# Leaf numbers of three routing trees: scattered to DRAM and spread by a DMA, in place of transposes on TensorE

## Chip, cores and metric

The kernel runs on one core of one Trainium2 chip. The metric is the device time of the core in microseconds; lower is better.

## What is computed

The input x is 4 x 512 tokens of width 128. The result is x + attention(xn) + ffn(xn) with xn = layernorm(x). The attention has 16 heads of width 8 and a bias by relative position. The other branch is a "fast feedforward" with four trees, q, k, v and f:

```python
def _fff(x, nw, nb, w1, b1, w2, b2, act):
    node = jnp.zeros(x.shape[:2], dtype=jnp.int32)
    for _ in range(DEPTH):                                  # 8 levels, 256 leaves
        logit = jnp.einsum('bsd,bsd->bs', x, nw[node]) + nb[node]
        node = 2 * node + 1 + (logit > 0).astype(jnp.int32)
    leaf = node - NN
    h = act(jnp.einsum('bsd,bsdl->bsl', x, w1[leaf]) + b1[leaf])   # 16 wide
    return jnp.einsum('bsl,bsld->bsd', h, w2[leaf]) + b2[leaf]

q, k, v = (_fff(xn2, ..., relu) for each of three trees)
y = xn2 + softmax(q k^T / sqrt(128)) v
ffn = y + _fff(y, f_..., gelu)
```

Each token takes a path through a tree to one of 256 leaves and is multiplied by the small matrices of that leaf.

## The kernel before, in words

**Leaves in blocks.** Eight leaves of 16 columns make a block of 128 columns, so a tree has 32 blocks. The tokens of a tree are sorted by block into at most 48 tiles of 128 rows (2048 tokens fill 16, and each block may leave one partly filled), and four tiles make a group: 12 groups a tree, 36 for the trees q, k and v (n = 0 to 35), 12 more for f. Within a tile every row is multiplied by its block's whole matrix, and the 16 columns of its own leaf are kept by a mask: the kernel needs for each row the leaf's number within the block (0 to 7, `part_of`), spread over all 128 partitions, since the hidden values lie there with columns on partitions and tokens along the free axis.

**Sorting.** GpSimd's `scatter(t)` (line 420) writes a tree's tokens to their slots in DRAM (`xs`) with 16 indirect DMAs of 128 rows each, a row being 128 values and, as the 129th, the leaf's number within the block (line 424 puts it into `xr[:, :, P]`). `xs` has two buffers, so tree 2 uses that of tree 0 and its scatter waits until the masks of tree 0 have been taken (line 423). GpSimd then goes on, in this order: scatter of trees 0 and 1, 32 indirect DMAs that fetch output biases (`gather_b2`), scatter of tree 2, 16 more of `gather_b2`, and then `gather(t)`, which adds each tree's results by indirect DMA (line 444) once its last store has landed.

**A group's stages** (`STAGE_AT`, line 73), each in a slot of its own:

- x: TensorE transposes the four tiles of rows (line 1185); ScalarE copies them out (line 885).
- h: TensorE multiplies them by the first matrices (line 1191); ScalarE adds the bias and applies the activation, to `hr` (line 890).
- m: TensorE transposes four tiles of the broadcast 129th column into PSUM bank 7 (lines 1193 to 1197, semaphore `mk`); VectorE compares it with `C_LEAF` and multiplies it by `hr`, to `hm` (line 739).
- y: TensorE multiplies `hm` by the second matrices into the same bank 7 (line 1201, `yy`); VectorE copies it out, to `yl` (line 744).

**The order of the work** is written out by hand as slots. An attention step (of 16, each four heads of one batch) has 20 slots; the stages of group n stand at the slots

```python
STAGE_AT = {"x": 0, "h": 2, "m": 3, "y": 5}
EVERY = 4
TREES_FROM, QK_FROM, ATT_FROM, ROUTE_FROM, F_FROM = -16, 131, 139, 174, 226
```

that is at 4n - 16 plus the stage's number, for the trees q, k and v. Slots -20 to -1 are a first step that holds only the row maxima of attention step 0. In a slot TensorE runs attention's scores (lines 1114, 1125 and 1127), at some slots the weighing of values (line 1137), and then the stage of a group that stands there; VectorE, ScalarE and TensorE all follow the same order, each its own instructions. Between two steps stands a seam: VectorE finishes the row maxima (line 707), TensorE transposes them (line 1152), VectorE subtracts them (line 713). The 16 maxima of a step run on VectorE, and TensorE may be two scores ahead.

**SP's queue** loads and stores for the groups, in `turn(n)` (line 279): rows of n+2 (line 268, waits for the mask of n), then four value loads that read the block numbers (line 273), then the weights of n+2 (four DMAs, line 277, wait for y of n), then the store of n (line 293, waits for `yl`). The rows go to `xl`, with two buffers. At a tree's first group it also waits for that tree's scatter.

Of the kernel before, what the change touches and what calls it, by code (L numbers as in the profile page):

```python
# [28 lines left out]
P = 128  # L29
# [87 lines left out]
def build(nc, x, wq, wk, wv, wp, bp, table, onehot, cf, cb, nw, nb, wl, b2, out):  # L117
# [3 lines left out]
    xs = [nc.dram_tensor(f"xs{t}", [TILES * P, ROW], F32).ap() for t in range(2)]  # L121
    ys = [nc.dram_tensor(f"ys{t}", [TILES * P, P], F32).ap() for t in range(NTREE)]

    ctx = ExitStack()
    with ctx:
        def sb(name, shape, dt=F32):
# [52 lines left out]
        part_of = sb("part_of", [P, NTREE + 1, NT], I32)  # L179
        ewc = sb("ewc", [P, NTREE + 1], I32)  # L180
# [9 lines left out]
        blks = path_bf[:, 2 * LEAVES:2 * LEAVES + 2 * (BLK + 2)].rearrange("p (h l) -> p h l", h=2)  # L190
        bitsT = flat(yt[:, 2]).bitcast(BF16).rearrange("p (h t) -> p h t", h=2)
# [26 lines left out]
            "d_ew0 d_ew1 d_ew2 d_ew3 d_x d_c d_w d_u d_b d_f d_z d_n d_sc tc pa oh hb pop nbt d_nb z_mx pl tab_in d_far aug lkc mxc "  # L218
# [8 lines left out]
        def _(sp):  # L227
# [21 lines left out]
            for t in range(2):  # L249
                sp.dma_start(xs[t].rearrange("(p a r) c -> p a (r c)", p=P, r=n),  # L250
                             zeros).then_inc(S["d_z"], 16)

# [25 lines left out]

            def turn(n, last):

                if n + 2 < last:
                    t = (n + 2) // GROUPS
                    if (n + 2) % GROUPS == 0:
                        sp.wait_ge(S[f"d_ew{t}"], 16)
                        sp.wait_ge(S["d_sc"], 16 * NT * (t + 1))
                    sp.wait_ge(S["mk"], n + 1 + CREDIT["mk"])
                    rows(n + 2)
                    block_of = blocks(n + 2)
                    sp.wait_ge(S["yy"], n + 1 + CREDIT["yy"])
                    weights(block_of, n % 2)  # L290
                t, m = divmod(n, GROUPS)
                sp.wait_ge(S["yl"], n + 1 + CREDIT["yl"])
                sp.dma_start(ys[t % NTREE][m * GT * P:(m + 1) * GT * P, :].rearrange("(t p) c -> p t c", p=P), yl[:]
                             ).then_inc(S["st"], 16)
# [3 lines left out]
            for n in range(2):  # L298
                rows(n)
                weights(blocks(n), n)  # L300
            for n in range(NTREE * GROUPS):
                turn(n, NTREE * GROUPS)
# [24 lines left out]
        def _(pool):  # L327
# [82 lines left out]
            def left_rows():  # L410

                settle(G.memset(left[:].rearrange("p a b -> p (a b)"), -1.0))
                settle(G.affine_select(left[:], left[:], [[-P, KT], [P, KT - 1]], ALU.is_ge, 0.0,
                                       base=P - SAT - 1, channel_multiplier=-1))
                pool.wait_ge(S["d_z"], 32)
                for k in range(2 * HG):
                    c = HR * (k // 2) + 25 + 3 * (k % 2)
                    G.tensor_copy(mx[:, :, c:c + 3], left[:]).then_inc(S["mxc"], 1)

            def scatter(t):  # L420
                pool.wait_ge(S["sl"], t + 1)
                if t >= 2:
                    pool.wait_ge(S["mk"], GROUPS * (t - 1) + CREDIT["mk"])
# [4 lines left out]
                pool.wait_ge(S["d_sc"], 16 * NT * (t + 1))  # L428

# [54 lines left out]
        def _(dve):  # L484
# [249 lines left out]
            def stage(k, n):  # L734
                if k == "m":
                    dve.wait_ge(S["mk"], n + 1 + CREDIT["mk"])
                    dve.wait_ge(S["hr"], n + 1 + CREDIT["hr"])
                    dve.wait_ge(S["yy"], n + CREDIT["yy"])
                    V.scalar_tensor_tensor(flat(hm[:]), bank(BB[k]), col(C_LEAF), flat(hr[:]), ALU.is_equal, ALU.mult  # L739
# [62 lines left out]
            dve.wait_ge(S["d_z"], 32)  # L802
# [170 lines left out]
        def _(pe):  # L973
# [204 lines left out]
            def stage(k, n, par):  # L1178
# [8 lines left out]
                elif k == "h":  # L1187
# [4 lines left out]
                    last.then_inc(S["hh"], 1)  # L1192
                elif k == "m":
# [4 lines left out]
                else:  # L1198
                    pe.wait_ge(S["hm"], n + 1 + CREDIT["hm"])
                    for i in range(GT):  # L1200
# [195 lines left out]
```

## Time and profile before

| | us |
|---|---|
| median of 3 runs (661.14 to 661.71) | 661.16 |
| the profiled execution, its own time | 663.95 |
| its span, first to last instruction | 662.2 |
| TensorE busy | 581.9 |
| VectorE busy | 413.3 |
| ScalarE busy | 349.2 |
| GpSimd busy | 273.0 |

All durations in the prediction are from this one profiled execution, whose own time is 2.8 us above the median. The tree stage runs from the first transposes of group 0 at 86.9 us to about 335 us; before it lie the layer norm, the routing of three trees and the first scatter. In the views, PE is TensorE's matmuls, PEld its weight loads, DVE VectorE, ACT ScalarE, POOL GpSimd and SP SyncE, whose DMA issues are marked SPq. L707 is line 707 of the kernel before. A timeline row gives start and duration in us, the engine, the line, the operation with the tiles written and read, the shape, how many instructions were merged, and in brackets the idle time ahead with what ended it.

### The profile page before, as it was taken

How to read it: one execution, taken by the hardware profiler on the slowest of the kernel's cores; microseconds unless marked ns; L12 is line 12 of the kernel's file. 1: busy time of each engine (PE TensorE's matmuls, PEld its weight loads, DVE VectorE, ACT ScalarE, POOL GpSimd, SP SyncE). 2: the span in 40 equal slices, each digit the busy share in tenths (PEclk: the TensorE clock that was granted, in tenths of full speed). 3: DMA queues.
4: the chain of work that ended last, by engine and by line, in shares of the span. 5: the costliest groups of instructions: out<-in, count | busy, mean ns of one | idle time of the engine just before them, and what ended most of it. 6: DMA issues, size and time to landing. Idle time of an engine off the chain costs nothing.

```text
span 662.2 us, 11736 instructions
## 1 busy us (share of the span) xinstructions
PE 581.9 (88%) x3641; PEld 409.5 (62%) x3641; DVE 413.3 (62%) x970; ACT 349.2 (53%) x738; POOL 273.0 (41%) x288
## 2 busy tenths in 40 slices
PE   2499878999999999999999999988598989987986
PEld 0344466768687868777766656665264767665653
DVE  3866667566676665666666665766867556746730
ACT  4533323656564646465565645423154968786633
POOL 7853576760657852840058100000077800000880
PEclk9899979999999999999999999988799999989988
DMA  7979968885768884885422100000043655632231
GB/s 213 261 174 196 301 160 214 215 225 140 209 190 216 174 207 130 187 189 156 129 36 36 26 1 0 1 1 1 1 116 69 116 132 132 173 104 58 33 65 31
DMA packets 108701, 83.05 MB, mean 125 GB/s; under 512 B 8680, under 2 KB 105840, under 8 KB 108640
## 3 DMA queue, kind: packets, MB, share of 16 engines
q1 hardware_dynamic: 93344, 69.68, 40.1%
q0 software_dynamic: 15104, 12.63, 10.4%
q8 instruction: 29, 0.48, 0.3%
q14 instruction: 32, 0.26, 0.1%
q10 hardware_dynamic: 192, 0.00, 0.0%
HBM read 57.91 MB, written 24.36 MB: 124 GB/s over the span
## 4 chain that ended last, share of the span: by engine, by line
PE 66%; DVE 11%; ACT 10%; issue 6%; DMA 3%; POOL 2%; SPq 2%; DVEq 0%; ACTq 0%
PE ps L1125 8%; PE ps L1137 8%; PE ps L1127 8%; PE ps L1114 7%; PE ps L1201 6%; PE ps L1191 6%; PE ps L1062 3%; DVE ps L707 3%; POOL xs L426 2%; PE ps L1244 2%; PE ps L1258 2%; ACT L879 2%; PE ps L1196 2%; ACT hr L890 2%; PE ps L1011 2%
## 5 line engine op out<-in xcount | busy, mean ns | idle before, releaser
L707 DVE CUSTOM_DVE_ANT_0 ps<-ps,strip 128x512 f32<-128x512 f32 x256 | 177.4, 699 | 111.3 <-PE ps L1114 106.1
L879 ACT ACTIVATE pt<-ps 128x512 f32<-128x512 f32 x256 | 150.5, 600 | 100.8 <-PE ps L1127 98.5
L1125 PE MATMUL ps<-qs,km 128*128 128x512 f32 x256 | 128.8, 503 | 8.6 <-ACT pt L879 7.5
L1114 PE MATMUL ps<-km,qs 128*128 128x512 f32 x256 | 111.7, 439 | 9.3 <-DVE mx L707 7.6
L431 POOL DMA_INDIRECT yt<-ys,slot x48 | 74.4, 1551 | 80.5 <-DMA ys<-yl 66.5
L890 ACT ACTIVATE hr<-ps,wt 128x128 f32<-128x128 f32 x192 | 54.8, 368 | 69.9 <-PE ps L1191 69.8
L1127 PE MATMUL ps<-u_lo,rev_r 128*128 128x220 f32 (+1 forms) x256 | 75.2, 294 | 0.0
L1127 PE MATMUL ps<-u_hi,rev_r 128*128 128x220 f32 (+1 forms) x256 | 73.8, 288 | 0.0
L1125 PEld LDWEIGHTS ps<-qs,km 128*128 128x128 f32 x256 | 49.9, 195 | 34.7 <-ACT pt L879 21.4
L1137 PE MATMUL ps<-pt,v_aug 128*32 128x512 f32 x512 | 69.9, 619 | 0.7 <-ACT pt L879 0.7
L426 POOL DMA_INDIRECT xs<-xr,slot x64 | 62.4, 975 | 19.7 <-issue 18.3
L1191 PEld LDWEIGHTS ps<-xTs,wt 128*128 128x128 f32 x384 | 48.3, 194 | 27.5 <-issue 20.6
L424 POOL CAST xr<-part_of 128x16 f32<-128x16 int32 x4 | 0.8, 212 | 151.4 <-DVE slot L643 126.6
L1114 PEld LDWEIGHTS ps<-km,qs 128*128 128x128 f32 x256 | 49.1, 193 | 19.5 <-DVE mx L707 13.5
L431 POOL DMA_INDIRECT xr<-ys,slot x16 | 24.8, 1553 | 86.0 <-DMA ys<-yl 81.4
L1191 PE MATMUL ps<-xTs,wt 128*128 128x128 f32 x384 | 54.6, 286 | 4.6 <-DMA wt<-in_wl 4.6
L1127 PEld LDWEIGHTS ps<-u_lo,rev_r 128*128 128x128 f32 x256 | 49.0, 192 | 11.4
L431 POOL DMA_INDIRECT yt<-in_b,leaf x48 | 45.6, 950 | 21.5 <-issue 14.0
L1127 PEld LDWEIGHTS ps<-u_hi,rev_r 128*128 128x128 f32 x256 | 50.1, 196 | 5.2 <-issue 4.1
L1201 PE MATMUL ps<-wt,hm 128*128 128x128 f32 x384 | 52.5, 281 | 0.6
L1201 PEld LDWEIGHTS ps<-wt,hm 128*128 128x128 f32 x384 | 50.2, 195 | 4.4 <-DVE hm L739 2.9
L739 DVE SCALAR_TENSOR_TENSOR hm<-ps,cst,hr 128x512 f32<-128x512 f32 x48 | 35.9, 749 | 17.1 <-ACT hr L890 11.2
(232 smaller groups left out, 891.5 us busy)
## 6 DMA issues: line engine op xcount, KB each, us to landing
wt<-in_wl SPq DMA_DIRECT2D x192, 128.5 KB
xl<-xs SPq DMA_DIRECT2D x48, 258.0 KB, 3.8
ys<-yl SPq DMA_DIRECT2D x48, 256.0 KB
xs<-mx SPq DMA_DIRECT2D x2, 3096.0 KB, 22.5
strip<-bias_bf SPq DMA_DIRECT2D x1, 3584.0 KB, 39.7
u_hi<-bias_hi SPq DMA_DIRECT2D x1, 2496.0 KB, 15.9
u_lo<-bias_lo SPq DMA_DIRECT2D x1, 2496.0 KB, 31.2
xs<-xr,slot POOLq DMA_INDIRECT x64
```

The lines of the kernel that those rows point to most:

```text
L426: pool.indirect_dma_start(out=xs[t % 2][:, :], out_offset=bass.IndirectOffsetOnAxis(ap=slot[:, t, k:k + 1], axis=0), in_=xr[:, k, :], in_o ...
L431: pool.indirect_dma_start(out=dst, out_offset=None, in_=src[:, :], in_offset=bass.IndirectOffsetOnAxis(ap=idx, axis=0), compute_op=op).the ...
L707: V.tensor_tensor_reduce(out=bank(u % 2), in0=bank(u % 2), in1=strip[:, HG * g + j, b0:b0 + NS], scale=1.0, scalar=LOWEST, op0=ALU.add, op ...
L739: V.scalar_tensor_tensor(flat(hm[:]), bank(BB[k]), col(C_LEAF), flat(hr[:]), ALU.is_equal, ALU.mult).then_inc(S["hm"], 1)
L879: A.activation(pt[:, kt % 2, j, :], bank(2 + u % 2), ACT.Exp).then_inc(S["ex"], 1)
L890: last = A.activation(hr[:, i, :], ps[:, BB[k], i * P:(i + 1) * P], ACT.Relu if n < NTREE * GROUPS else ACT.Gelu, bias=wt[:, par, i, 2 * P ...
L1114: T.matmul(bank(u % 2), qs[:, par, qt * P:(qt + 1) * P], backward(km[:, par, j, :]), start=True, stop=True).then_inc(S["p1"], 1)
L1125: T.matmul(bank(2 + u % 2), km[:, par, j, kt * P:(kt + 1) * P], qs[:, par, :], start=True, stop=False)
L1127: last = T.matmul(ps[:, 2 + u % 2, lo:hi], rev_r[:], half[:, HG * g + j, u0:u0 + hi - lo], start=False, stop=stop)
L1137: last = T.matmul(ps[HR * j:HR * j + HR, OB, :], v_aug[:, par, kt, j, :], pt[:, kt % 2, j, :], start=kt == 0, stop=kt == KT - 1)
L1191: last = T.matmul(quarter(BB[k], i), wt[:, par, i, 0:P], xTs[:, i, :], start=True, stop=True)
L1201: last = T.matmul(quarter(BB[k], i), hm[:, i, :], wt[:, par, i, P:2 * P], start=True, stop=True)
```

## The change

For the trees q, k and v the leaf's number no longer takes the way over TensorE. GpSimd writes the numbers, as bf16, with 16 more indirect DMAs a tree (2 bytes for each token) to a row in DRAM, `leaf_row[t]`, which SP has zeroed before. For each group SP loads 512 numbers of this row into all 128 partitions at once (`leaf_at`, one buffer, on the bytes of `b_pT`), and VectorE's instruction for `hm` reads them there. The stage m on TensorE is empty for these groups. Tree f keeps the transposes. Waits on `mk` become waits on `xT` (the row transposes are done) where only the read of the rows mattered; y takes over the wait for `yl`.

```diff
+    leaf_row = [nc.dram_tensor(f"leaf_row{t}", [TILES * P, 1], BF16).ap() for t in range(NTREE)]
...
+        part_bf = sb("part_bf", [P, NT], BF16)
...
+        leaf_at = path_bf[:, 0:GT * P]
...
+            for t in range(NTREE):
+                sp.dma_start(leaf_row[t].rearrange("(p a) one -> p (a one)", p=P), flat(mx[:]).bitcast(BF16)[:, 0:TILES]
+                             ).then_inc(S["d_z"], 16)
...
+            def leaves(n):
+
+                t, m = divmod(n, GROUPS)
+                sp.wait_ge(S["d_sl"], 16 * NT * (t + 1))
+                sp.dma_start(leaf_at, bass.AP(tensor=leaf_row[t].tensor, offset=m * GT * P, ap=[[0, P], [1, GT * P]])
+                             ).then_inc(S["d_at"], 16)
+
             def turn(n, last):
 
                 if n + 2 < last:
...
-                    sp.wait_ge(S["mk"], n + 1 + CREDIT["mk"])
+                    sp.wait_ge(S["xT"], n + 1)
+                    if n >= NTREE * GROUPS:
+                        sp.wait_ge(S["mk"], n - NTREE * GROUPS + 1 + CREDIT["mk"])
                     rows(n + 2)
                     block_of = blocks(n + 2)
+                if n + 1 < NTREE * GROUPS:
+                    sp.wait_ge(S["hm"], n + 1 + CREDIT["hm"])
+                    leaves(n + 1)
+                if n + 2 < last:
                     sp.wait_ge(S["yy"], n + 1 + CREDIT["yy"])
                     weights(block_of, n % 2)
...
             for n in range(2):
                 rows(n)
                 weights(blocks(n), n)
+            sp.wait_ge(S["hb"], NTREE)
+            leaves(0)
             for n in range(NTREE * GROUPS):
                 turn(n, NTREE * GROUPS)
...
-                pool.wait_ge(S["d_z"], 32)
+                pool.wait_ge(S["d_z"], 16 * (2 + NTREE))
...
             def scatter(t):
                 pool.wait_ge(S["sl"], t + 1)
                 if t >= 2:
-                    pool.wait_ge(S["mk"], GROUPS * (t - 1) + CREDIT["mk"])
+                    pool.wait_ge(S["xT"], GROUPS * (t - 1))
                 settle(G.tensor_copy(xr[:, :, P], part_of[:, t, :]))
                 for k in range(NT):
                     pool.indirect_dma_start(out=xs[t % 2][:, :], out_offset=bass.IndirectOffsetOnAxis(ap=slot[:, t, k:k + 1], axis=0),
                                             in_=xr[:, k, :], in_offset=None).then_inc(S["d_sc"], 16)
                 pool.wait_ge(S["d_sc"], 16 * NT * (t + 1))
+                if t < NTREE:
+                    settle(G.tensor_copy(part_bf[:], part_of[:, t, :]))
+                    for k in range(NT):
+                        pool.indirect_dma_start(out=leaf_row[t][:, :], out_offset=bass.IndirectOffsetOnAxis(ap=slot[:, t, k:k + 1], axis=0),
+                                                in_=part_bf[:, k:k + 1], in_offset=None).then_inc(S["d_sl"], 16)
+                    pool.wait_ge(S["d_sl"], 16 * NT * (t + 1))
...
             def stage(k, n):
                 if k == "m":
-                    dve.wait_ge(S["mk"], n + 1 + CREDIT["mk"])
+                    if n < NTREE * GROUPS:
+                        dve.wait_ge(S["d_at"], 16 * (n + 1))
+                    else:
+                        dve.wait_ge(S["mk"], n - NTREE * GROUPS + 1 + CREDIT["mk"])
                     dve.wait_ge(S["hr"], n + 1 + CREDIT["hr"])
                     dve.wait_ge(S["yy"], n + CREDIT["yy"])
-                    V.scalar_tensor_tensor(flat(hm[:]), bank(BB[k]), col(C_LEAF), flat(hr[:]), ALU.is_equal, ALU.mult
+                    V.scalar_tensor_tensor(flat(hm[:]), leaf_at if n < NTREE * GROUPS else bank(BB[k]), col(C_LEAF), flat(hr[:]), ALU.is_equal, ALU.mult
                                            ).then_inc(S["hm"], 1)
...
-            dve.wait_ge(S["d_z"], 32)
+            dve.wait_ge(S["d_z"], 16 * (2 + NTREE))
...
+                elif k == "m" and n < NTREE * GROUPS:
+                    pass
                 elif k == "m":
                     pe.wait_ge(S["yl"], n + CREDIT["yl"])
...
                 else:
                     pe.wait_ge(S["hm"], n + 1 + CREDIT["hm"])
+                    pe.wait_ge(S["yl"], n + CREDIT["yl"])
```

## Rows read from the trace of the kernel before

**Rows 1.** The page: busy time of each engine, and the granted clock in 40 slices

```profile
PE 581.9 (88%) x3641; PEld 409.5 (62%) x3641; DVE 413.3 (62%) x970; ACT 349.2 (53%) x738; POOL 273.0 (41%) x288
...
PEclk9899979999999999999999999988799999989988
```

**Rows 2.** Busy time of each engine in one stretch of the tree stage

```profile
core 0: us, PE busy (x) PEld busy (x) DVE busy (x) ACT busy (x) POOL busy (x), PEclk, DMA share, GB/s
130.00:200.00 70.00, 68.66 (x479) 52.23 (x479) 45.29 (x105) 38.95 (x94) 34.29 (x38) 1.00 0.71 190
```

**Rows 3.** Timeline of 138 to 146 us, TensorE and VectorE, groups 7 and 8

```profile
139.75 0.70 DVE L707 CUSTOM_DVE_ANT_0 ps<-ps,strip 128x512 f32<-128x512 f32 x1 [2.02 <-PE ps L1114]
...
140.37 0.75 DVE L739 SCALAR_TENSOR_TENSOR hm<-ps,cst,hr 128x512 f32<-128x512 f32 x1
...
141.17 1.16 PE L1201 MATMUL ps<-wt,hm 128*128 128x128 f32 x8
...
144.72 0.60 PE L1196 MATMUL ps<-cst,xl 128*128 128x128 f32 x4
...
145.89 0.66 PE L1152 MATMUL ps<-cst,mx 128*128 128x128 f32 x4 [0.57 <-DVE mx L707]
145.92 0.75 DVE L739 SCALAR_TENSOR_TENSOR hm<-ps,cst,hr 128x512 f32<-128x512 f32 x1
```

**Rows 4.** Timeline of TensorE alone, inside a step

```profile
125.94 0.60 PE L1196 MATMUL ps<-cst,xl 128*128 128x128 f32 x4
126.30 0.48 PE L1125 MATMUL ps<-qs,km 128*128 128x512 f32 x1
```

**Rows 5.** Groups by line, VectorE: two elementwise instructions over 512 columns

```profile
L713 DVE TENSOR_TENSOR qs<-qs,ps 128x512 fp32r<-128x512 f32 x16 | 10.9, 682 | 3.8 <-PE ps L1152 3.7
...
L641 DVE TENSOR_TENSOR pt<-pt 128x512 f32<-128x512 f32 x3 | 2.1, 692 | 0.1
```

**Rows 6.** Timeline of GpSimd: the second scatter of rows

```profile
82.61 0.21 POOL L424 CAST xr<-part_of 128x16 f32<-128x16 int32 x1 [3.99 <-DMA xs<-xr,slot]
83.10 0.98 POOL L426 DMA_INDIRECT xs<-xr,slot  x1 [0.28 <-POOL xr L424]
...
102.17 0.96 POOL L426 DMA_INDIRECT xs<-xr,slot  x1 [0.30 <-issue]
106.57 1.00 POOL L431 DMA_INDIRECT yt<-in_b,leaf  x1 [3.43 <-DMA xs<-xr,slot]
```

**Rows 7.** DMA issues of the whole run, then those of 86 to 112 us: last column us to landing

```profile
xTs<-in_nw SPq DMA_DIRECT2D x1, 128.0 KB, 2.3
xTs<-in_nb SPq DMA_DIRECT2D x1, 128.0 KB, 3.2
...
xl<-xs SPq DMA_DIRECT2D x4, 258.0 KB, 4.6
```

**Rows 8.** Timeline of VectorE: hm of groups 0 and 2

```profile
95.69 0.75 DVE L739 SCALAR_TENSOR_TENSOR hm<-ps,cst,hr 128x512 f32<-128x512 f32 x1
...
106.34 0.75 DVE L739 SCALAR_TENSOR_TENSOR hm<-ps,cst,hr 128x512 f32<-128x512 f32 x1
```

**Rows 9.** List of waits, 112 to 340 us: engine waited for, us in total, times, longest

```profile
POOL yt L431 <- DMA ys<-yl: 66.5, 2, 47.4
...
POOL xr L424 <- PE ps L1196: 20.8, 1, 20.8
```

**Rows 10.** Timeline of SP's DMA issues: first step, then around group 7

```profile
100.99 0.56 SPq L268 DMA_DIRECT2D xl<-xs  x1
104.64 1.93 SPq L277 DMA_DIRECT2D wt<-in_wl  x4
...
138.51 0.43 SPq L293 DMA_DIRECT2D ys<-yl  x1
140.03 0.38 SPq L268 DMA_DIRECT2D xl<-xs  x1
142.80 1.93 SPq L277 DMA_DIRECT2D wt<-in_wl  x4
```

More of the change, by code:

```diff
@@ L217, in build @@
         S = {n: ctx.enter_context(nc.semaphore(n)) for n in (
-            "d_ew0 d_ew1 d_ew2 d_ew3 d_x d_c d_w d_u d_b d_f d_z d_n d_sc tc pa oh hb pop nbt d_nb z_mx pl tab_in d_far aug lkc mxc "
+            "d_ew0 d_ew1 d_ew2 d_ew3 d_x d_c d_w d_u d_b d_f d_z d_n d_sc tc pa oh hb pop nbt d_nb d_sl d_at z_mx pl tab_in d_far aug lkc mxc "
             "sl tick rt_in rt_out ones ln_m ln_r ln_sub ln_sq ln_out xT_ps xT_sb xnT_sb tab_ps tab_sb v_ps v_sb lg bit oh5 rk rt id wsc "
```

## The prediction

> **What bounds the kernel now.** I read the page first: TensorE is busy 581.9 us of 662.2 [rows 1]. That is an average, so I then read the busy time of a stretch of the tree stage, where the change acts: from 130 to 200 us TensorE is busy 68.66 of 70 us, at a granted clock of 1.00 (its 2.4 GHz level), while VectorE has 45.29 and ScalarE 38.95 [rows 2]. There TensorE is the bound, and an instruction taken from it can shorten the run. The timeline around the seam between two attention steps shows the exception: TensorE idles 0.57 us before the transposes of the row maxima (line 1152), because VectorE's last maximum isn't ready [rows 3]. The same happens at each seam of the tree stage.
>
> Durations below are of the profiled execution (663.95 us, span 662.2, so 1.75 lie outside the span). The median of the runs is 661.16, 2.8 lower; I put the sum on the median.
>
> **What is removed.** Each of the 36 groups of trees 0 to 2 loses four transposes on TensorE. The four start at 125.94 and the next matmul at 126.30: 0.355 us a group [rows 4]. All 36 would be 12.8 us, but not all count. The mask stage of group n stands at slot 4n - 13 and a step has 20 slots, so the groups fall into kinds. In groups 8, 13, 18, 23, 28 and 33 the mask transposes stand last in a step: in group 8 they start at 144.72, and behind them line 1152 waits for the maximum until 145.89 [rows 3]. Without them it waits the longer, so the gain is 0. In groups 7, 12, 17, 22, 27 and 32 VectorE computes hm at 140.37, straight behind the maximum that began at 139.75, and TensorE's second matmul (line 1201) starts at 141.17, once hm is done [rows 3]. What holds hm there is VectorE's own order, not the transposes: gain 0. Groups 0 to 3 lie in the first attention step, where VectorE and the weight loads set the pace: gain 0. The other 20 give 20 x 0.355 = **-7.1 us**. The bounds are -12.8 (all 36 count) and -5 (some third of the 20 goes back into waits for VectorE and ScalarE).
>
> The instruction for hm now reads bf16 from SBUF in place of f32 from PSUM. An elementwise instruction over 512 columns takes 692 ns with both tensors in SBUF and 682 with one in PSUM [rows 5], so this is priced at 0. The Trainium skill (VectorE: DVE Perf Modes, section "The TRN2 errata") gives 58 + FD cycles from SBUF and 120 + FD from PSUM. By that each hm would be 65 ns shorter, an estimate, and the sum some 0.8 us lower over the twelve groups where hm is on the path. The rows show nothing of it.
>
> **What is added on GpSimd.** Behind each scatter of rows now stand a cast, 16 more indirect DMAs and a wait for their landing. The second row scatter is the model: cast at 82.61, DMAs from 83.10 to 102.17 (1.27 us apart), and the instruction after the wait at 106.57, in all 24.0 us [rows 6]. In the changed kernel this block for tree 0 stands exactly where the second scatter stood, so its leaf numbers are in DRAM at 106.6, and SP can't load them before. The load that spreads them (128 partitions x 1 KB) lands 2.3 us after its issue (as a plain 128 KB load did), 3.2 (as a row broadcast to all partitions) or 4.6 (as the loads of xl at this time) [rows 7]. I take 3.5, near the broadcast, since the second row scatter then runs beside it. hm of group 0 started at 95.69 [rows 8]. Now it starts at 110.1: **+14.4 us** (13.2 to 15.5). Queued behind this wait on VectorE are the row maxima of the first step, and TensorE, at most two scores ahead of them, stands still too. The slots are one order on every engine, so nothing later fills the hole. TensorE will have the transposes of group 1 and a score or two done by then: **-0.5**. It comes back from the hole at the lower clock; the page grants 0.7 in the slice from 83 to 99 us already [rows 1], so such a dip is paid for in this place before, and I count 0, at most +2.
>
> The page DMA: Bandwidth & Descriptors of the Trainium skill (section "Anatomy of one DMA") fits a DMA with 2.0 us + bytes / 436 GB/s, for those issued from GpSimd. For 128 KB that is 2.3 us, an estimate. By it this term would be 1.2 us less. The broadcast row's 3.2 us speaks against it.
>
> The later blocks cost nothing by themselves. GpSimd gets 3 x 24 = 72 us more in all. It waits 20.8 us before the third scatter (which will now start once x of tree 0 is read, not its mask), and 66.5 us in two waits before the gathers of trees 1 and 2 [rows 9]: 87.3 us of cover, so the gather of tree 2 still starts when the last ys lands. If this cover were gone, the q and k transposes at slot 131 would be late.
>
> **What is added on SP.** A turn is now: rows n+2, four value loads, leaf numbers n+1 (new, behind hm of n), weights n+2 (behind yy of n), store n. The new issue takes 0.4 us, mostly inside the wait for yy. But it can't go before the value loads are done. In steady state the store is issued at 138.51 for 0.43 us, the rows take 0.38, and the value loads 2.4 (from the end of the rows' issue at 140.41 to the weights at 142.80, at most) [rows 10]. So the leaf numbers of group 8 go out at 141.8 and land at 145.3, where its hm started at 145.92 [rows 3]: 0.6 us to spare, with landings of 2.3 to 4.6 us. For the six groups of this kind I put **+0.6** in all (0 to 4). In the first step the groups are closer and the value loads slower: the rows' issue ends at 101.55 and the weights start at 104.64 [rows 10]. The leaf numbers of group 2 would be issued there and land at 108.1, where hm of group 2 started at 106.34 [rows 8]: **+1.8** (0 to 4).
>
> Zeroing the leaf rows (three small DMAs behind those of xs, and the longer wait for them) is priced at 0: the long loads of the bias strips follow, and nothing waits for the zeros before them. The leaf loads' bytes (36 x 128 KB, in a stage that uses 0.71 of the DMA engines' time [rows 2]) are in the bounds of the landings.
>
> **Sum:** 14.4 - 0.5 + 1.8 + 0.6 - 7.1 = **+9.2 us**, so 661.16 + 9.2 = 670.4 us.
>
> **Rivals.** First, the leaf load becomes the wait of every seam and of the first step: SP's chain of weights, store, rows, value loads, leaf issue and landing is longer than the pace. For it speak the 0.6 us of spare and one issue more in each turn; against it, that this is the shortest of the five intervals in a step. It decides where landing takes over 4.1 us. At 5 us it costs 6 x 0.9 more at the seams and some 3 in the first step, +8 on my sum: 678.6 us. Chance 0.13.
>
> Second, the transposes' whole price comes back (12.8), with the shortest stall (13.2) and no late leaf load: 13.2 - 0.5 - 12.8 = -0.1, no change, 661.1 us. Against it stand the idle time before line 1152 and the start of hm in group 7 [rows 3]. Chance 0.07.
>
> Third, on the other side, GpSimd issues DMAs of 2-byte elements quicker than those of 516-byte rows. At 0.95 us apart (the idle 0.3 us between two gone) the block takes 16 x 0.32 = 5.1 us less, the stall falls to 9.3, and if the transposes' whole price comes back as well the sum is 9.3 - 0.5 - 12.8 = -4.0: 657.2 us. It decides below some 1.15 us a DMA. Against it: the 1.27 us held over all of the second scatter [rows 6]. Chance 0.05.
>
> **Numbers.** My forecast has the other 0.75. The range of 665 to 677 takes its bounds (13.2 - 0.5 - 8.9 = +3.8 at the low end, 15.5 + 2 + 4 - 5.5 = +16 at the high end) and leaves out the rivals' ends. A measurement of this kernel can tell about 0.2% (1.3 us) from no change. Slower by more than that: 0.88; within it 0.07; faster 0.05.
>
> **What would show it.** VectorE's first hm at about 110 us, after some 14 us more of idle time than before, ended by the DMA of leaf numbers; TensorE with as long a hole; GpSimd's DMAs of leaf numbers 1.27 us apart; the time from the first hm of tree 1 to the last of tree 2 shorter by 20 x 0.355 in proportion, less what the seams give back. I am wrong if the hole is under 12 us, if hm at seams waits for the leaf load by over 1 us each, or if the tree stage shortens by over 9 us.

## The result, and the profile after

| | before | after |
|---|---|---|
| median of the runs, us | 661.15 | 692.54 (4 runs, 687.14 to 698.09) |
| ratio, 95% interval | | 1.0442 (1.04 to 1.0484) |
| profiled execution, us | 663.95 | 691.88 |
| its span, us | 662.2 | 690.1 |
| first hm, us from the start | 95.7 | 109.2 |
| first hm to that of group 35 | 235.8 | 250.3 |
| hm of group 35 to that of group 36 (tree f) | 186.3 | 186.3 |

The change makes the kernel 4.4% slower, 31.4 us on the medians, where 9.2 were forecast. One of its four runs, the one of 698.09 us, is slow and is left out of the ratio, which puts the loss at 29 us (26 to 32). The profiled executions are 27.9 us apart. 13.5 of these lie before the first hm and 14.5 between the first hm and that of group 35. Behind the tree stage nothing is lost.

The page of the changed kernel: busy time, granted clock, packets and the chain that ended last, to be held against [rows 1].

```profile
PE 579.3 (84%) x3497; PEld 398.3 (58%) x3497; DVE 413.6 (60%) x970; ACT 346.3 (50%) x738; POOL 322.5 (47%) x339
...
PEclk9999966899999999999999999999889999999998
...
DMA packets 115854, 87.82 MB, mean 127 GB/s; under 512 B 11224, under 2 KB 112992, under 8 KB 115792
...
PE 39%; POOL 15%; issue 11%; DVE 10%; ACT 9%; DMA 8%; SPq 7%; DVEq 0%; ACTq 0%; POOLq 0%
```

TensorE has 144 matmuls fewer (36 groups of four), and yet only 2.6 us less of busy time: part of what is left runs at a lower clock, in slices of 0.6, 0.6 and 0.8 between 86 and 138 us.

The busy time by stretch of the changed kernel. The columns are those of [rows 2], the number ahead of the last two is the granted clock.

```profile
core 0: us, PE busy (x) PEld busy (x) DVE busy (x) ACT busy (x) POOL busy (x), PEclk, DMA share, GB/s
98.00:110.00 12.00, 0.00 (x0) 0.00 (x0) 0.80 (x2) 0.02 (x1) 8.07 (x10) 0.50 0.40 75
110.00:115.00 5.00, 4.99 (x19) 4.25 (x19) 2.79 (x8) 0.74 (x3) 3.78 (x5) 0.50 0.49 130
...
125.00:130.00 5.00, 4.00 (x18) 3.40 (x18) 2.79 (x8) 1.14 (x4) 0.95 (x1) 0.59 0.87 181
...
130.00:200.00 70.00, 64.30 (x414) 46.59 (x413) 42.91 (x99) 37.19 (x89) 48.69 (x52) 0.98 0.79 194
```

For 12 us TensorE does nothing. Then it works at its 1.2 GHz level. From 130 to 200 us it is busy 64.30 of 70 us where it was busy 68.66 [rows 2]: it is no longer the bound throughout, and the DMA engines' share has gone from 0.71 to 0.79.

The start of the tree stage, from the timelines of GpSimd alone and of all engines:

```profile
83.21 0.20 POOL L451 CAST part_bf<-part_of 128x16 bf16<-128x16 int32 x1 [4.16 <-DMA xs<-xr,slot]
83.69 0.96 POOL L453 DMA_INDIRECT leaf_row<-part_bf,slot  x1 [0.28 <-POOL part_bf L451]
84.95 0.96 POOL L453 DMA_INDIRECT leaf_row<-part_bf,slot  x1 [0.30 <-issue]
...
102.64 0.95 POOL L453 DMA_INDIRECT leaf_row<-part_bf,slot  x1 [0.30 <-issue]
105.11 0.21 POOL L445 CAST xr<-part_of 128x16 f32<-128x16 int32 x1 [1.52 <-DMA leaf_row<-part_bf,slot]
105.12 0.33 SPq L289 DMA_DIRECT2D b_pT<-leaf_row  x1
...
109.20 0.75 DVE L769 SCALAR_TENSOR_TENSOR hm<-b_pT,cst,hr 128x512 f32<-128x512 bf16 x1 [13.38 <-DMA b_pT<-leaf_row]
...
110.01 2.08 PE L1234 MATMUL ps<-wt,hm 128*128 128x128 f32 x8 [12.20 <-DVE hm L769]
```

That is the forecast hole: 16 DMAs 1.26 us apart, the load behind them, and hm at 109.20 instead of 95.69 [rows 8].

Next, VectorE's list of waits over the tree stage (84 to 380 us), and SP's issues around group 10, where no scatter runs:

```profile
DVE hm L769 <- DMA b_pT<-leaf_row: 30.2, 14, 13.4
DVE yl L774 <- DMA ys<-yl: 27.9, 25, 3.0
DVE hm L769 <- ACT hr L920: 9.3, 6, 1.9
```

```profile
181.06 0.44 SPq L312 DMA_DIRECT2D ys<-yl  x1
181.61 0.43 SPq L274 DMA_DIRECT2D xl<-xs  x1
184.67 0.33 SPq L289 DMA_DIRECT2D b_pT<-leaf_row  x1
185.19 1.92 SPq L283 DMA_DIRECT2D wt<-in_wl  x4
```

Besides the hole hm waits 30.2 - 13.4 = 16.8 us for the leaf loads, in 13 groups. And the copy to `yl`, which needs the store before it to have landed, waits 27.9 us; the kernel before has 9.6 in 13 waits in its own tree stage (84 to 352 us). The leaf load goes out 2.63 us behind the end of the rows' issue (181.61 + 0.43), that is behind the value loads.

Two of the waits for the loads, in groups 5 and 13, in VectorE's timeline. The load of group 5 was issued at 142.04, beside the second leaf scatter (131.2 to 151.4 us):

```profile
147.97 0.75 DVE L769 SCALAR_TENSOR_TENSOR hm<-b_pT,cst,hr 128x512 f32<-128x512 bf16 x1 [2.55 <-DMA b_pT<-leaf_row]
...
201.55 0.75 DVE L769 SCALAR_TENSOR_TENSOR hm<-b_pT,cst,hr 128x512 f32<-128x512 bf16 x1 [1.04 <-DMA b_pT<-leaf_row]
```

In the changed kernel's trace the last packet of a leaf load ends 2.6 to 3.9 us after the issue where no leaf scatter runs beside it (4.0 and 4.8 in two groups, 3 and 2), and 4.0 to 6.2 us after it in groups 4 to 6 and 17 to 19, beside one.

### The profile page after: what moved, and what is told of

It reads as the page before. It is cut to its first block, busy times and chain, and to the rows that moved or that the text cites. A ratio compares the mean times of both kernels' runs of the same rounds, so it can differ in the third digit from the quotient of the medians.

```text
span 690.1 us, 11632 instructions
## 1 busy us (share of the span) xinstructions
PE 579.3 (84%) x3497; PEld 398.3 (58%) x3497; DVE 413.6 (60%) x970; ACT 346.3 (50%) x738; POOL 322.5 (47%) x339
## 4 chain that ended last, share of the span: by engine, by line
PE 39%; POOL 15%; issue 11%; DVE 10%; ACT 9%; DMA 8%; SPq 7%; DVEq 0%; ACTq 0%; POOLq 0%
POOL xs L447 6%; PE ps L1155 5%; PE ps L1167 5%; POOL yt L458 4%; PE ps L1157 4%; POOL leaf_row L453 4%; PE ps L1144 4%; SPq L279 3%; SPq L283 3%; DVE ps L734 3%; PE ps L1234 2%; PE ps L1092 2%; DMA xs<-xr,slot 2%; PE ps L1277 2%; PE ps L1291 2%
## 5 line engine op out<-in xcount | busy, mean ns | idle before, releaser
L458 POOL DMA_INDIRECT yt<-ys,slot x48 | 74.8, 1559 | 52.4 <-DMA ys<-yl 33.9
L1234 PE MATMUL ps<-wt,hm 128*128 128x128 f32 x384 | 55.2, 289 | 20.9 <-DVE hm L769 20.4
L1221 PEld LDWEIGHTS ps<-xTs,wt 128*128 128x128 f32 x384 | 50.2, 200 | 26.3 <-issue 19.6
L1144 PEld LDWEIGHTS ps<-km,qs 128*128 128x128 f32 x256 | 49.3, 196 | 21.5 <-DVE mx L734 15.5
L458 POOL DMA_INDIRECT yt<-in_b,leaf x48 | 47.0, 980 | 24.7 <-issue 14.0
L1221 PE MATMUL ps<-xTs,wt 128*128 128x128 f32 x384 | 56.1, 292 | 2.9 <-DMA wt<-in_wl 2.8
L774 DVE COPY yl<-ps 128x512 f32<-128x512 f32 x48 | 33.2, 691 | 37.5 <-DMA ys<-yl 29.2
```

The source lines that it names most:

```text
L458: pool.indirect_dma_start(out=dst, out_offset=None, in_=src[:, :], in_offset=bass.IndirectOffsetOnAxis(ap=idx, axis=0), compute_op=op).the ...
L774: V.tensor_copy(flat(yl[:]), bank(BB[k])).then_inc(S["yl"], 1)
L1144: T.matmul(bank(u % 2), qs[:, par, qt * P:(qt + 1) * P], backward(km[:, par, j, :]), start=True, stop=True).then_inc(S["p1"], 1)
L1221: last = T.matmul(quarter(BB[k], i), wt[:, par, i, 0:P], xTs[:, i, :], start=True, stop=True)
L1234: last = T.matmul(quarter(BB[k], i), hm[:, i, :], wt[:, par, i, P:2 * P], start=True, stop=True)
```

## The experiments

Each run is compared with the kernel before on the same chip. **Stage** below is the time from the first hm to that of group 35, from the profiled execution. The chips of these runs gave medians of 658.4 to 660.0 for the kernel before, with single runs from 656 to 666.5 (and one of 3,099, which is left out of everything). In all runs but e4, e9 and e11 the masks are left out: hm compares either with the bytes that happen to lie in the buffer (e1, e2, e5, e6), with zeros (e3, e7, e8, e10, e13), or with a row of zeros of its own for each partition (e12).

| | median | ratio, 95% | first hm | stage | hm waits for leaf load | yl waits for store |
|---|---|---|---|---|---|---|
| before | | 1 | 95.7 | 235.8 | | 9.6 |
| after | 692.54 | 1.044 (1.040 to 1.048) | 109.2 | 250.3 | 30.2 | 27.9 |
| e1 gain alone | 654.66 | 0.993 (0.991 to 0.996) | 93.7 | 230.6 | | 13.5 |
| e2 + scatters | 661.45 | 1.002 (0.999 to 1.006) | 94.3 | 237.2 | | 26.2 |
| e3 + loads | 668.51 | 1.016 (1.013 to 1.019) | 96.2 | 240.4 | 11.0 | 18.1 |
| e4 two buffers | 680.0 | 1.034 (1.031 to 1.037) | 107.2 | 239.1 | 17.1 | 37.5 |
| e5 = e2, 512 B apart | 655.15 | 0.992 (0.989 to 0.995) | 94.2 | 231.3 | | 12.4 |
| e6 = e2, 64 B each | 653.52 | 0.989 (0.986 to 0.992) | 94.2 | 229.7 | | 15.1 |
| e7 = e3, two buffers | 661.41 | 1.003 (1.000 to 1.006) | 97.6 | 234.6 | 4.3 | 20.9 |
| e8 = e7, from ScalarE | 661.03 | 1.002 (0.999 to 1.005) | 92.8 | 235.1 | 0.8 | 43.1 |
| e9 tree q transposed | 659.53 | 1.001 (0.997 to 1.004) | 94.5 | 237.8 | 1.5 | 27.3 |
| e10 after, 512 B apart | 680.78 | 1.032 (1.027 to 1.036) | 108.6 | 243.6 | 25.1 | 17.1 |
| e11 after again | 684.03 | 1.039 (1.034 to 1.045) | 108.3 | 247.0 | 36.0 | 28.3 |
| e12 = e7, distinct rows | 661.49 | 1.004 (1.001 to 1.006) | 94.4 | 235.1 | 2.6 | 20.1 |
| e13 = e7 again | 662.12 | 1.004 (1.001 to 1.007) | 97.4 | 233.9 | 4.9 | 16.8 |

The waits are those of VectorE from 84 to 380 us (before: to 352). Among the kernels without a hole the first hm lies anywhere from 92.8 to 97.6 us (in e3, e7, e12 and e13 it waits 2.6 to 3.3 us for the first leaf load), so I read the stage. Each stage is one execution. The same kernel taken twice gave 250.3 and 247.0 (after and e11), and 234.6 and 233.9 (e7 and e13), so one pair of stages doesn't settle a difference of 3 us.

### The parts of the change

e1_gain_alone: the change without leaf scatters and without loads.

```diff
-                if t < NTREE:
-                    settle(G.tensor_copy(part_bf[:], part_of[:, t, :]))
...
-                if n + 1 < NTREE * GROUPS:
-                    sp.wait_ge(S["hm"], n + 1 + CREDIT["hm"])
-                    leaves(n + 1)
...
-                        dve.wait_ge(S["d_at"], 16 * (n + 1))
+                        dve.wait_ge(S["tc"], 1)
```

> The mask transposes of trees q, k and v are gone from TensorE and nothing is put in their place: no leaf scatters, no leaf loads, no wait for them (hm compares with bytes that happen to lie in SBUF, so the mask of these trees is left out). It measures what the removal is worth by itself. By the step of my prediction (20 groups of 36 count): -7 us, 654. By the rival of the whole price: -12.8 us, 648. If something else paces the stage (SP's queue, the landing of the stores): -3 or less.

e2_plus_scatters: the first of these three cuts is taken back; nobody reads the leaf rows or waits for them.

> As e1, with the zeroing and the 48 scatters of leaf numbers on GpSimd put back, which nobody waits for. By my prediction, and by the theory that only the loads matter: the same as e1 within 1 us, since GpSimd has 87 us of cover. By the theory that small writes slow all other DMAs: 3 to 10 us above e1.

e3_plus_loads: the loads and their waits are back, the scatters are out, and `leaves` waits for the zeros in place of the scatter.

> As e1, with the 36 leaf loads on SP put back, one buffer, behind the value loads as in the change, and VectorE waiting for them, but no scatters: they read the zeros of the leaf rows. There is no hole at the start. Theory queue (the place in SP's order, the issue time and the load's own landing make leaf numbers and stores late): 15 to 22 us above e1, with over 10 us of waits of hm for the load and over 20 us of waits of yl for stores. Theory scatter (the loads are late because small scatters run beside them): at most 5 us above e1.

Removing the transposes shortens the stage by 5.2 us. The scatters, which nobody waits for, cost 6.6 us of it (237.2 against 230.6), the loads with their waits 9.8 (240.4). With -5.2 + 6.6 + 9.8 the stage would be 247.0; the changed kernel has 250.3, so 3.3 us are left over, by subtraction (3.2 if taken from the 14.5). On the medians of this chip e2 is 6.8 and e3 13.9 us over e1, and 2.5 of the 13.9 lie before the first hm. So e2 fell in the range of small writes that slow other DMAs, and e3 between its two theories (15 to 22, or at most 5).

The cost of the scatters isn't spread evenly. Against e1, e2 is 4.6 us late by hm of group 4, loses nothing in groups 5 to 20, though the second leaf scatter runs there too (131.7 to 151 us), and loses the other 2.0 in groups 21 to 24, beside the third.

For the scatters the DMA view of 92 to 100 us shows the mechanism. First e1, then e2, in the same stretch:

```profile
DMA packets 1790, 1.62 MB, mean 202 GB/s; under 512 B 208, under 2 KB 1709, under 8 KB 1790
## 3 DMA queue, kind: packets, MB, share of 16 engines
q1 hardware_dynamic: 1629, 1.28, 65.2%
q0 software_dynamic: 161, 0.33, 11.0%
...
xs<-xr,slot POOLq DMA_INDIRECT x7
```

```profile
DMA packets 1584, 0.99 MB, mean 124 GB/s; under 512 B 352, under 2 KB 1583, under 8 KB 1583
## 3 DMA queue, kind: packets, MB, share of 16 engines
q1 hardware_dynamic: 1331, 0.98, 92.9%
q0 software_dynamic: 193, 0.00, 1.7%
...
leaf_row<-part_bf,slot POOLq DMA_INDIRECT x7
```

In e1 the seven indirect DMAs are rows of 516 bytes, and SP's transfers (q1) take 65% of the engines' time for 1.28 MB. In e2 they are leaf numbers of 2 bytes, and SP's transfers take 93% for 0.98 MB. The scatter's own packets use 1.7%. So it isn't the scatter that fills the engines: the transfers beside it slow down. The mean weight packet (1,028 bytes) starting in this stretch takes 69 ns in e1 and 142 in e2; beside the second leaf scatter (131 to 152 us) it is 55 and 83, beside the third (220 to 243) 62 and 119.

### Is it the density of the small writes?

e5_scatter_spread: e2 with the same 2-byte writes, 512 bytes apart in a larger array.

```diff
-    leaf_row = [nc.dram_tensor(f"leaf_row{t}", [TILES * P, 1], BF16).ap() for t in range(NTREE)]
+    leaf_row = [nc.dram_tensor(f"leaf_row{t}", [TILES * P * 256, 1], BF16).ap() for t in range(NTREE)]
...
+                    settle(G.tensor_scalar(slot_w, slot[:, t, :], 256.0, None, ALU.mult))
...
-                        pool.indirect_dma_start(out=leaf_row[t][:, :], out_offset=bass.IndirectOffsetOnAxis(ap=slot[:, t, k:k + 1], axis=0),
+                        pool.indirect_dma_start(out=leaf_row[t][:, :], out_offset=bass.IndirectOffsetOnAxis(ap=slot_w[:, k:k + 1], axis=0),
```

> As e2 (scatters that nobody waits for, no loads), but the 2-byte numbers go to slots 512 bytes apart in DRAM in place of 2 bytes apart. e2 was 6.8 us over e1, and the weight loads' 1028-byte packets took about 142 ns beside the first leaf scatter against 69 in e1. Theory size (each 2-byte write to DRAM costs the other DMAs): the same as e2, +1 us on the kernel before, packets over 110 ns. Theory place (the writes of a tree all fall into 12 KB of DRAM, and hold up what shares it): the same as e1, -5 us, packets near 70 ns. Theory GpSimd (its later gathers and scatters are what costs): as e2, but with packets as in e1.

e6_scatter_64B: e2 with dense elements of 64 bytes.

```diff
-    leaf_row = [nc.dram_tensor(f"leaf_row{t}", [TILES * P, 1], BF16).ap() for t in range(NTREE)]
+    leaf_row = [nc.dram_tensor(f"leaf_row{t}", [TILES * P, 16], F32).ap() for t in range(NTREE)]
...
-                                                in_=part_bf[:, k:k + 1], in_offset=None).then_inc(S["d_sl"], 16)
+                                                in_=xr[:, k, 0:16], in_offset=None).then_inc(S["d_sl"], 16)
```

> As e2, but each element is 64 bytes (16 columns of the row) and the target 393 KB a tree. Theory size: cheaper than e2, near e1 (-5 us on the kernel before) if it's writes under 64 bytes that cost. Theory place: near e1 too, and e5 near e1. Theory GpSimd: as e2.

With the same number of DMAs at the same pace the cost is gone in both: stages of 231.3 and 229.7 against 230.6 without any scatter. The same DMA view of e5, which has e2's order of DMAs on GpSimd and so is the fairer pair for it:

```profile
DMA packets 2142, 1.46 MB, mean 182 GB/s; under 512 B 334, under 2 KB 2142, under 8 KB 2142
## 3 DMA queue, kind: packets, MB, share of 16 engines
q1 hardware_dynamic: 1952, 1.45, 65.9%
q0 software_dynamic: 190, 0.00, 1.7%
```

SP's transfers take 66% of the engines' time for 1.45 MB. The mean weight packet is back at 57 ns (63 in e6). So it was the crowding of 2-byte writes into 12 KB a tree, not their number and not GpSimd's time. Whether the writes collide within a few bytes or within a larger region isn't told apart: both edits end either.

### What the loads cost

e4_two_buffers: the whole change, with two leaf buffers, and the load of n+1 behind hm of n-1 and ahead of the value loads.

```diff
-        leaf_at = path_bf[:, 0:GT * P]
+        leaf_at = [path_bf[:, i * GT * P:(i + 1) * GT * P] for i in range(2)]
...
                     rows(n + 2)
-                    block_of = blocks(n + 2)
                 if n + 1 < NTREE * GROUPS:
-                    sp.wait_ge(S["hm"], n + 1 + CREDIT["hm"])
+                    sp.wait_ge(S["hm"], n + CREDIT["hm"])
                     leaves(n + 1)
                 if n + 2 < last:
+                    block_of = blocks(n + 2)
```

> The whole change, but with two buffers for the leaf numbers: the load for group n+1 needs only hm of n-1 and is issued ahead of the value loads of a turn. The hole of 13.5 us at the start stays. Both theories: hm waits no longer for the load outside the start (14 us of waits gone). If those waits are what the tree stage lost: about 14 us under the change, 678. If the stores' late landing paces the stage (SP's chain is as long as before): at most 5 us under the change, 687 or more.

The stage falls from 250.3 to 239.1 (from 247.0 if e11 is taken): 8 to 11 us go with one buffer more and another place in SP's queue. The median, 680.0, is near the 678 that were expected if those waits are what the stage lost. What is left of hm's wait, 17.1 us, is the hole (14.06) and 3.0 more. Now the stores are the wait, 37.5 us for `yl`.

e7_loads_two_buffers is e3 with the same edit.

> As e3 (loads and waits, no scatters), with two buffers and the load ahead of the value loads. e3 was 13.9 us over e1. Theory late leaf numbers: most of it comes back, +1 us or less on the kernel before, and hm doesn't wait for the load. Theory queue length (0.37 us more on SP in each turn makes weights and stores late): +5 us or more on the kernel before.

e8_loads_on_scalar issues e7's loads from ScalarE's queue, so that SP's is as long as in e1.

```diff
+                    if n + 1 < NTREE * GROUPS:
+                        leaves(n + 1)
...
-                sp.dma_start(leaf_at[n % 2], bass.AP(tensor=leaf_row[t].tensor, offset=m * GT * P, ap=[[0, P], [1, GT * P]])
+                act.dma_start(leaf_at[n % 2], bass.AP(tensor=leaf_row[t].tensor, offset=m * GT * P, ap=[[0, P], [1, GT * P]])
```

> As e7_loads_two_buffers, but the 36 loads are issued from ScalarE's queue, behind the stage h of the group before. SP's turn is then as in e1. Theory queue length: 4 us or more under e7_loads_two_buffers, and yl waits less for stores. Theory traffic (128 KB more a group is what costs, whoever issues it): within 1.5 us of it. ScalarE pays some 0.4 us a group, which has room (52% busy).

So the 9.8 us of e3 are two things: 5.8 go with the second buffer and the earlier issue (240.4 to 234.6) and 4.0 stay (234.6 against e1's 230.6; on the ratios 0.94%, 6.2 us). The 4.0 stay when ScalarE issues the loads (235.1): SP's longer queue isn't it. The Trainium skill (DMA: Bandwidth & Descriptors, section "Issuing engines are not separate DMA queues") says that DMAs of all issuing engines run on the same 16 engines and that another queue saves only the time to issue them. By that e8 should equal e7, and it does, 661.03 against 661.41 us. The other half of my expectation, shorter waits of `yl` if SP's queue was it, came out the other way: they grew to 43.1 us, at no cost in time. These waits aren't a measure of what is lost.

e12_loads_distinct reads 128 different rows of 1 KB in place of one row 128 times; e13_loads_again is e7 on the same chip.

```diff
-    leaf_row = [nc.dram_tensor(f"leaf_row{t}", [TILES * P, 1], BF16).ap() for t in range(NTREE)]
+    leaf_row = [nc.dram_tensor(f"leaf_row{t}", [P, GT * P], BF16).ap() for t in range(NTREE)]
...
-                sp.dma_start(leaf_at[n % 2], bass.AP(tensor=leaf_row[t].tensor, offset=m * GT * P, ap=[[0, P], [1, GT * P]])
+                sp.dma_start(leaf_at[n % 2], leaf_row[t]
```

> As e7_loads_two_buffers (no leaf scatters, two buffers, load ahead of the value loads, masks left out), but each load reads 128 different rows of 1 KB (a 128-KB array of zeros) in place of one row read 128 times. Bytes, packets and queue are the same. If 128 reads of one place are what makes the loads dear, this comes to e1's 0.993 of before (first hm to hm of group 35 near 231 us). If it is the traffic itself, or the issue and the wait, it stays with e13 of this call, near 1.003 (234 to 236 us).

> e7_loads_two_buffers unchanged, for a comparison on the same chip as e12: 1.003 of before, within 0.003; first hm to hm of group 35 at 234 to 236 us.

661.49 against 662.12 us: it isn't the one place that all partitions read. What remains is that 36 x 128 KB more are moved, and hm's need of them. From 96 to 326 us the DMA share is 0.73 in e1 and 0.81 in e13:

```profile
96.00:326.00 230.00, 214.60 (x1423) 159.45 (x1423) 154.19 (x355) 126.76 (x308) 119.06 (x103) 1.00 0.73 186
```

```profile
96.00:326.00 230.00, 211.18 (x1386) 157.73 (x1387) 151.74 (x349) 123.29 (x300) 119.87 (x104) 0.99 0.81 206
```

So there is more traffic, but no run took the bytes away and kept the loads, and that traffic is the cause isn't shown. Where the time is lost speaks in part against it: by hm of group 4, e7 is 2.8 us behind e1, e12 3.3, e13 1.8 and e8 1.7, and from group 4 to group 23 e7 and e12 lose nothing more (e13 and e8 1.5), with the same loads beside them. The larger part falls in the first step, behind a first hm that waited 3.3, 2.6, 3.2 and 0.8 us for its load. What it is stays open.

### The two halves together

e10_change_spread is the change with the scatter as in e5, to an array of its own; the loads read the zeroed row. e11_change_again is the change, on the same chip.

```diff
+    leaf_far = [nc.dram_tensor(f"leaf_far{t}", [TILES * P * 256, 1], BF16).ap() for t in range(NTREE)]
...
-                        pool.indirect_dma_start(out=leaf_row[t][:, :], out_offset=bass.IndirectOffsetOnAxis(ap=slot[:, t, k:k + 1], axis=0),
+                        pool.indirect_dma_start(out=leaf_far[t][:, :], out_offset=bass.IndirectOffsetOnAxis(ap=slot_w[:, k:k + 1], axis=0),
```

> The change as it is, but the 2-byte numbers are scattered to slots 512 bytes apart in another DRAM tensor, while the leaf loads read the zeroed row (the mask of these trees is left out). All waits and all counts of DMAs are those of the change. By the theory of the place (dense 2-byte writes slow the loads beside them): 8 to 12 us under the change in the same call, leaf packets at 60 to 80 ns throughout, in place of 200 to 400 beside scatters. By the theory that the waits and the one buffer are all: within 3 us of it.

> The change once more, on the same chip as e9 and e10, for their comparison: 29 to 32 us over the kernel before.

e10 stays under what the theory of the place promised (8 to 12 us): it is 3.3 us under e11 on the medians and 3.4 in the stage (247.0 to 243.6), at the edge of the other expectation, and no more than two profiles of one kernel differ. What the trace does show is the packets. In e11 those of the leaf loads beside a leaf scatter (groups 4 to 6 and 17 to 19) take 161 to 468 ns in the mean of a load, and over all loads 122; in e10 over all loads 78. e11 itself missed its expectation: 24.8 us over the kernel before where 29 to 32 were expected. Its stage of 247.0 is no longer than the sum of the parts, and the changed kernel's first profile is 4.4 us behind it before group 6 alone. So the 3.3 us left over rest on one profile, and an effect of the two halves on each other isn't shown. Also, e10's stage is 3.2 us over e3's, and 2.1 of that lie before group 6, right behind the hole (42.3 against 40.25 us from the first hm). There a clock of 0.50 is granted from 108 to 113 us and again from 123 to 128:

```profile
core 0: us, PE busy (x) PEld busy (x) DVE busy (x) ACT busy (x) POOL busy (x), PEclk, DMA share, GB/s
108.00:113.00 5.00, 3.59 (x16) 3.50 (x17) 3.42 (x8) 0.00 (x0) 3.83 (x4) 0.50 0.53 126
...
123.00:128.00 5.00, 4.00 (x17) 3.39 (x17) 2.79 (x8) 1.14 (x4) 2.06 (x3) 0.50 0.75 201
```

### A version without the hole

e9_tree0_transposed: e4, but tree q keeps its transposes (`VIA` = 12 groups), so no leaf scatter stands ahead of the first hm.

```diff
-                if t < NTREE:
+                if 0 < t < NTREE:
...
-                elif k == "m" and n < NTREE * GROUPS:
+                elif k == "m" and VIA <= n < NTREE * GROUPS:
```

> The change with two buffers (e4), but tree q keeps its transposes on TensorE; only trees k and v take the way over DRAM. e4 was 20 us over the kernel before. By the theory that the hole at the start (11.5 us there) and the first scatter's cost to the weight loads beside it (4.6 of the 6.6 us of e2) are all of it: hm of group 0 is back near 95 us, the run lands within 2 us of the kernel before, 658 to 662. If scatters and loads cost as much in the later trees as in the first: 4 us or more above it.

The hole is gone (first hm at 94.5) and the median is that of the kernel before: 1.001 (0.997 to 1.004). hm waits 1.5 us in all for the loads, `yl` 27.3 for its stores. That is what was expected (658 to 662) if the hole and the first scatter's cost are all of it. (The profiled execution was the slowest of twelve, 664.58 us, so its stage of 237.8 is on the long side.) The gain of 24 groups without transposes is eaten, by e2 and e7 by the dense scatters and the loads; here they weren't parted. No version that takes the masks beats the kernel before. A scatter of 64-byte elements would need a load that picks 2 bytes out of every 64, which wasn't tried.

## Why the prediction was wrong

**Start hole.** Forecast +14.4 (13.2 to 15.5), measured +13.5. The 1.27 us between DMAs held (1.26). Two errors cancel in part: the leaf numbers were in DRAM at 105.1 and not 106.6, since after the last DMA the wait was 1.5 us and not 3.4; the load took 4.1 us to hm and not 3.5. The estimate of 2.3 us from the Trainium skill (DMA: Bandwidth & Descriptors, section "Anatomy of one DMA") was further off. Where hm stalls in the hole also agrees: VectorE, then TensorE.

**Transposes removed.** Forecast -7.1 with bounds of -12.8 and -5; e1 gives -5.2 of stage and -4.4 on the ratio (-2.7 to -6.0). That not all 36 count was right, and the bound of -5 is what happened. The count was off: from group 8 on, each step of five groups gives 0.7 to 0.9 us, two groups' worth, where three were counted, and it shows in hm of groups 12, 17, 22, 27 and 32 and of the two before each, though the first of these kinds had been put at 0. The waits between 100 and 330 us show where the rest went. First the kernel before, then e1:

```profile
PE ps L1152 <- DVE mx L707: 4.1, 7, 0.7
PE ps L1185 <- ACT hr L890: 0.4, 1, 0.4
```

```profile
PE ps L1171 <- DVE mx L723: 7.6, 7, 1.4
PE ps L1204 <- ACT hr L909: 2.4, 6, 0.4
```

TensorE waits 3.5 us more for the row maxima and 2.0 more for ScalarE.

**hm from SBUF, priced at 0.** The instruction takes 751 ns, before 750. The 65 ns less that were estimated from the Trainium skill (VectorE: DVE Perf Modes, section "The TRN2 errata") aren't seen here.

**"The later blocks cost nothing by themselves."** This step failed. The cover held: GpSimd still waited 33.9 us for a store before a gather, late in the stage, and e5 and e6 have the same DMAs on GpSimd at no cost. But I looked for the cost of the scatters on GpSimd alone, and it lay in the DMA engines: +6.6 us by e2, from transfers of SP that slow down while 2-byte writes crowd into 12 KB. e5 and e6 show that it is this. The first block has this cost too (4.6 of the 6.6 us lie before hm of group 4 in e2, which has no hole). No row of the trace before has such writes, so this cost had to be bounded by a row of another transfer beside a scatter, and it had no bound at all.

**Leaf loads, +1.8 and +0.6.** This step failed in size. The seams cost more than their bound: at the six of them e3 waits 5.3 us in all (0.55, 1.64, 0, 0.35, 1.83 and 0.94 in groups 8, 13, 18, 23, 28 and 33), where 0.6 with a bound of 4 was written. But with one buffer the load can go only behind the hm before it and the value loads, so it is the wait in the first step too (groups 2, 4 and 5 in the changed kernel: 2.83, 1.85 and 2.55 us, where only group 2 was priced). e3 less e7 puts the late issue at 5.8 us, where 2.4 were forecast; only 0.2 of the 5.8 lie before hm of group 4, so without scatters it is the seams and not the first step that pay.

**"The leaf loads' bytes are in the bounds of the landings."** This failed: 4.0 us of stage remain in e7 (3.3 to 4.5 in e13, e8 and e12) that no term of the sum holds. hm waits for its loads only 4.3 us there, and 3.3 of them lie before the stage. As much remains on the other queue (e8) and with distinct rows (e12). Whether it is the bytes stays open.

**Clock after the hole, priced at 0, at most +2.** The granted clock was 0.50 from 98 to 115 us and 0.59 from 125 to 130, and the eight matmuls of y took 2.08 us for 1.16 [rows 3]. [Rows 1] had a dip there before, but a shorter one. e3, without a hole, also has 0.52 in the first 5 us of its stage. e10 against e3 puts the aftermath of the hole at some 2.1 us before group 6, e4 against e7 at 0.8 (40.85 and 40.02 us), so its size is open, and no run parts the clock from other causes in it.

**The rivals.** The first (a leaf load that becomes the wait at every seam and in the first step, 678.6 us) had its mechanism partly right, but its condition, a landing over 4.1 us, held only in groups 5, 6 and 17 to 19, beside leaf scatters, and in group 2. The second (the whole price of the transposes back) falls with e1, the third (quicker 2-byte DMAs) with the 1.26 us.

**The range.** 665 to 677 was built with -8.9 and -5.5 for the transposes, where the bounds given were -12.8 and -5, and with one of the two bounds of 4 us for late loads. With the bounds as given the high end is 15.5 - 0.5 + 2 + 4 + 4 - 5 = +20.0, 681 us, and still misses.

**The sum as measured**, on the profiles: 13.5 - 5.2 + 6.6 + 5.8 + 4.0 + 3.3 = 28.0 against 27.9 between the two executions. It closes because 3.3 is what was left over. The terms without an entry in the forecast are 6.6, shown to be one transfer slowing another, 4.0, whose cause is open, and 3.3, which the second profile of the changed kernel doesn't have. On the medians the loss is 31.4, 3.5 more, since the profiled execution of before lay 2.8 us above its median and that of the changed kernel 0.7 below.

## What to carry to other kernels

When work moves from an engine to DMA in a stage where the DMA engines are already 0.7 busy, count what the new transfers do to those that are there, and test it by adding the transfers with nobody waiting for them. Don't write small elements (2 bytes here) densely to DRAM beside other traffic: pad them or spread them. A load in a loop that is issued behind the use of its own buffer can arrive too late for the next use; the second buffer with the earlier issue was worth 5.8 us here (e3 to e7), more than the 5.2 of the edit that the loads served.

## What the runs showed of the hardware that was not expected

- 2-byte indirect writes, 2,048 to a 12-KB array at 128 in each 1.26 us, doubled the time of 1,028-byte weight packets beside them (69 to 142 ns; 55 to 83 and 62 to 119 beside the two later scatters) and went with 216 to 410 ns for the 1-KB packets of leaf loads beside them (the means of groups 4 to 6 and 17 to 19 in the changed kernel), where 26 of the other 30 loads have 45 to 142. The other four (groups 0, 3, 15 and 16) have 202 to 246, three of them with no leaf scatter beside them (that of 16 ends 1.8 us into the third), which stays open. In e4, where the loads go ahead, those beside leaf scatters have only 45 to 217. At 512 bytes apart, or with elements of 64 bytes, the effect on the weights was gone (57 and 63 ns).
- Their landing can be slow too. The DMA view of the changed kernel from 140 to 148 us, where the last column is the time from issue to landing in us:

```profile
ys<-yl SPq DMA_DIRECT2D x1, 256.0 KB, 6.7
leaf_row<-part_bf,slot POOLq DMA_INDIRECT x8, 5.6
```

  A DMA of 256 bytes takes 5.6 us, and the store beside it 6.7, where the changed kernel's stores have a median of 4.1.
  In the stretch from 98 to 104 us, where TensorE stands still and SP's transfers take 25% of the engines' time, the same DMAs take 2.9 us.
- A load that replicates one 1-KB row to 128 partitions costs the same as one of 128 different rows (e12 and e13: 661.49 and 662.12 us).
